# A stage border reordered: spikes counted by five comparisons, one fill moved to GpSimd, the first projections in two banks

## The chip, the cores and the metric

The kernel runs on one core of one Trainium2 chip. The metric is the device time of one launch in microseconds (us), as the median of several runs; lower is better. TensorE (PE) does the matrix products, VectorE (DVE), ScalarE (ACT) and GpSimd (POOL) work elementwise, and SyncE (SP) issues the transfers.

## What is computed

The input `x` has 8 sequences of 1024 tokens with 512 features. The cut reference:

```python
xn = layernorm(x)
# attention, 16 heads of 32, on xn
q, k, v = xn @ Wq.T, xn @ Wk.T, xn @ Wv.T
attn = softmax(q @ k.T * 512**-0.5) + rel_bias        # bias is added after the softmax
s = layernorm(attn @ v) * ln_gamma + ln_beta
# feed forward with spiking neurons, on xn
h = relu(xn @ W_fc.T) ** 2
y = h @ W_proj.T
mem = 0
for _ in range(5):
    mem = 0.9 * mem + y - (mem > 1)
    spikes += (mem > 1)
g = silu(spikes / 5)
out = x + s * g
```

## The kernel before, in words

The program has three stages, one after the other, each a block in which the five engines run their own queues in order; between blocks all engines meet.

**Weights** (`prepare_weights`). The weights are loaded, scaled and split in a high and a low half-precision part, so that three half-precision products (`TERMS`) stand for one of full precision.

**Feed forward** (`feed_forward`). The 8192 tokens go in 16 chunks (`NC`) of 512. In a chunk a loop over `f` (16 steps) runs a product with `w_fc` (L434, 12 matmuls of 512 columns), ScalarE's ReLU (L514), VectorE's square (L581), ScalarE's high part (L500), VectorE's low part (L586) and, two steps later, the product with `w_pr` into four banks (L447). ScalarE then copies `y` to memory (`copy_y`, L527). Beside that, the next chunk is loaded (`x_in`, L384), normalised, transposed and split into `xnT_part`, which SyncE stores to `xnT` in DRAM (L391), with a copy of the bias table (L399). The **recurrence** of a chunk takes 14 VectorE steps (`SpikingGate.recurrence`), each on all 2048 elements of a partition: L82, L84, L86, then L90, L92, L94 in turn, and last L98, the product of the spike count and the sigmoid. The sigmoid is three ScalarE instructions, `Exp`, `Ln`, `Exp` (L106, L110, L112). The recurrence of chunk c-1 runs in the steps `f` = 3 to 15 of chunk c; its sigmoid and its gate run in chunk c+1, and SyncE then stores the gate (L72). So at the end of the stage the sigmoid and gate of chunk 14 and the whole recurrence of chunk 15 are left over.

**Attention** (`attention`). The work goes in slots, one for each group of four heads of a sequence (32 slots, g = 0 to 31), each of 32 half steps `h`. A slot weighs the values of its own group (L978 scores transposed, L1042 ScalarE's exponential, L1294 GpSimd's bias, L993 product with the values) while the same slot prepares the next group: tiles of plain scores (L967), their row maximum on VectorE (`row_max`, L1101) and their exponential with row sums on ScalarE (`exp_sum`, L1048), 32 tiles a group. It also projects queries and keys two groups ahead (`project_qk`, L925, four units u = 0 to 3 of 12 matmuls of 512 columns) and values one group ahead (`project_v`, L908, two units of 48 matmuls of 128 columns). All projections go through one PSUM bank, `misc`: VectorE empties it (`take_qk`: L1135 writes the high part, L1137 the low one; `take_v`: L1107) before TensorE may start the next (`take_misc`, `last_use`). Once the four units of a group are read, SyncE spreads `nat` over `qst` and `kst` with 24 transfers (L853, six for each head), on which the score tiles wait (`stacked`).

Two slots in front, g = -2 and g = -1, fill this pipeline: slot -2 only projects queries and keys of group 0; slot -1 projects the values of group 0 and the queries and keys of group 1, and takes the first 26 tiles of group 0. What is left over of the spiking gate stands in them: ahead of the slots VectorE's four constants (`subT`, `before_key`, `identh`, and the ones in `kst`, L1255), the seven fills of `before_key` (L1258), for which TensorE waits before its first matmul (`CONSTS`), and the gate of chunk 14; in the slots the 13 steps of chunk 15 by the table

```python
RECURRENCES = {(-2, 17): (0, 1), (-2, 19): (2, 3), (-2, 23): (4, 5), (-2, 27): (6, 7), (-2, 31): (8,),
               (-1, 0): (9,), (-1, 2): (10,), (-1, 4): (11,), (-1, 5): (12,), (-1, 12): (13,)}
```

in which (g, h) says where a step stands in VectorE's queue. The order of every queue is the order of the code: each engine walks `slot` over its own steps. SyncE loads `xT` (L804), the normalised and transposed tokens of a whole sequence, at the start of the stage.

## Time and profile before

| | us |
|---|---|
| median of 3 runs (lowest to highest) | 3731.57 (3731.06 to 3733.22) |
| the profiled execution's own time | 3732.06 |
| its span | 3730.3 |
| PE busy | 3529.2 |
| DVE busy | 2738.0 |
| ACT busy | 2687.1 |
| POOL busy | 1577.9 |

The profile is one execution. Its span runs from the first to the last instruction; the execution's own time is 1.8 us longer. A busy TensorE is one with matmuls in flight, at whichever clock. Busy shares are averages over three stages, so they say little of any one of them; stretches of the span are read apart.

### The profile page before, as it was taken

What the parts mean: (1) busy time and instruction counts of PE and PEld (TensorE: products, weight loads), DVE (VectorE), ACT (ScalarE), POOL (GpSimd) and SP (SyncE); (2) the same over time, 40 slices, a digit from 0 to 9 for tenths busy, and PEclk for the clock granted to TensorE, in tenths of its full rate; (3) what the DMA queues carried; (4) which work ended last, traced back from release to release, by engine and by line L of the source; (5) the groups of instructions that cost most, each with busy time, mean ns of one, the idle gap of its engine ahead of it and who ended that gap; (6) DMA issues with size and microseconds to landing.
All of it is one profiled execution on the core that took longest, in us unless ns stands there. A gap on an engine that the chain in (4) does not pass through costs nothing.

```text
span 3730.3 us, 57349 instructions
## 1 busy us (share of the span) xinstructions
PE 3529.2 (95%) x20204; PEld 1498.2 (40%) x20204; DVE 2738.0 (73%) x4090; ACT 2687.1 (72%) x4941; POOL 1577.9 (42%) x898
## 2 busy tenths in 40 slices
PE   3999999999999996899999999999999999999985
PEld 1444444444444443343343343433433434334331
DVE  5376666666667667777877877778787787787776
ACT  4233333333433332999999999999999999999994
POOL 1000000000000000367677776776777767767766
PEclk6999999999999998999999999999999999999997
DMA  4011111111111102122232231232322322232221
GB/s 171 29 41 41 41 41 41 41 44 66 41 48 45 41 29 71 55 57 87 80 102 75 80 115 58 89 106 74 89 88 78 94 80 86 86 96 82 75 74 63
DMA packets 141421, 261.03 MB, mean 70 GB/s; under 512 B 19248, under 2 KB 52784, under 8 KB 140624
## 3 DMA queue, kind: packets, MB, share of 16 engines
q1 hardware_dynamic: 141136, 257.37, 21.9%
q8 instruction: 162, 2.65, 0.3%
q14 instruction: 123, 1.01, 0.1%
HBM read 155.77 MB, written 59.83 MB: 58 GB/s over the span
## 4 chain that ended last, share of the span: by engine, by line
ACT 38%; issue 18%; DVE 3%; PE 2%; ACTq 0%; POOL 0%; SPq 0%; DMA 0%; DVEq 0%
ACT recurrence_or_probs L1042 25%; ACT s_sb L1048 13%; PE st_ps L978 1%; PE acc L993 0%; DVE s_sb L1101 0%; ACTq L44 0%; PE s_ps L967 0%; DVE recurrence_or_probs L90 0%; PE misc L936 0%; PE misc L925 0%; DVE kst L1255 0%; DVE recurrence_or_probs L94 0%; DVE recurrence_or_probs L92 0%; DVE nat L1135 0%; DVE gate_or_tokens L1187 0%
## 5 line engine op out<-in xcount | busy, mean ns | idle before, releaser
L1101 DVE TENSOR_SCALAR_CACHE_REDUCE s_sb<-s_ps 128x1024 f32<-128x1024 f32 x1024 | 1244.6, 1222 | 424.0 <-PE s_ps L967 394.0
L1294 POOL TENSOR_TENSOR recurrence_or_probs<-recurrence_or_probs,toep 128x2048 f32<-128x2048 f32 (+3 forms) x384 | 1321.7, 3459 | 301.1 <-ACT recurrence_or_probs L1042 301.1
L1048 ACT ACTIVATE s_sb<-s_sb,nmax 128x1024 f32<-128x1024 f32 x1024 | 1270.1, 1240 | 7.2 <-DVE s_sb L1101 6.6
L1042 ACT ACTIVATE recurrence_or_probs<-st_ps 128x512 f32<-128x512 f32 x2048 | 1188.9, 678 | 16.3 <-PE st_ps L978 16.3
L978 PE MATMUL st_ps<-qst,kst 99*128 99x512 f16 x2048 | 677.7, 387 | 60.6 <-ACT recurrence_or_probs L1042 44.3
L434 PE MATMUL ps_fc<-xnT_part,w_fc 128*128 128x512 f16 x3072 | 706.1, 380 | 1.4 <-DVE xnT_part L573 1.4
L447 PE MATMUL ps_y<-w_pr,hid_part 128*128 128x512 f16 x3072 | 704.5, 379 | 0.0
L514 ACT ACTIVATE relu<-ps_fc 128x512 f32<-128x512 f32 x256 | 152.9, 597 | 733.1 <-PE ps_fc L434 733.1
L967 PE MATMUL s_ps<-kst,qst 96*128 96x512 f16 x2048 | 614.2, 381 | 8.9 <-DVE s_sb L1101 8.9
L1329 POOL MEMSET unit<- 128x16 f32 x1 | 0.1, 112 | 1408.3 <-POOLq L329 1408.3
L993 PE MATMUL acc<-recurrence_or_probs,val 128*32 128x512 f32 x4096 | 549.1, 609 | 4.6 <-POOL recurrence_or_probs L1294 4.6
L581 DVE TENSOR_TENSOR hid<-relu 128x512 f32<-128x512 f32 x256 | 177.1, 692 | 453.4 <-ACT relu L514 453.4
L978 PEld LDWEIGHTS st_ps<-qst,kst 99*128 99x128 f16 x2048 | 195.7, 98 | 707.7 <-ACT recurrence_or_probs L1042 598.9
L447 PEld LDWEIGHTS ps_y<-w_pr,hid_part 128*128 128x128 f16 x3072 | 300.6, 98 | 362.5
L434 PEld LDWEIGHTS ps_fc<-xnT_part,w_fc 128*128 128x128 f16 x3072 | 300.9, 98 | 351.8 <-issue 2.2
L1048 ACT ACTIVATION_READ_ACCUMULATOR s_sb<-s_sb,nmax 128x1 f32 x1024 | 298.4, 291 | 0.0
L500 ACT ACTIVATE hid_part<-hid 128x512 f16<-128x512 f32 x256 | 160.7, 628 | 160.8 <-DVE hid L581 160.8
L967 PEld LDWEIGHTS s_ps<-kst,qst 96*128 96x128 f16 x2048 | 199.8, 98 | 149.6 <-DVE s_sb L1101 11.2
L908 PE MATMUL misc<-w_v,xT 128*128 128x128 f16 x3072 | 194.8, 220 | 10.8 <-DVE val L1107 9.3
L925 PE MATMUL misc<-xT,w_q 128*128 128x512 f16 x768 | 190.1, 384 | 13.0 <-DVE before_key L1258 10.8
L908 PEld LDWEIGHTS misc<-w_v,xT 128*128 128x128 f16 x3072 | 184.2, 98 | 42.2 <-DVE val L1107 9.5
L925 PE MATMUL misc<-xT,w_k 128*128 128x512 f16 x768 | 188.2, 381 | 8.4 <-DVE nat L1137 6.6
(117 smaller groups left out, 2542.9 us busy)
## 6 DMA issues: line engine op xcount, KB each, us to landing
toep<-table_rows SPq DMA_DIRECT2D x32, 2048.0 KB, 8.1
qst<-nat SPq DMA_DIRECT2D x384, 64.0 KB, 2.0
kst<-nat SPq DMA_DIRECT2D x384, 64.0 KB, 2.0
x_in<-in_x SPq DMA_DIRECT2D x16, 1024.0 KB, 7.3
xnT<-xnT_part SPq DMA_DIRECT2D x32, 512.0 KB, 4.3
gate<-gate_or_tokens SPq DMA_DIRECT2D x16, 1024.0 KB, 4.3
xT<-xnT SPq DMA_DIRECT2D x32, 512.0 KB, 9.7
x_or_gate<-gate SPq DMA_DIRECT2D x64, 256.0 KB, 2.9
```

Of the source, the lines that this page charges most:

```text
L434: last = nc.tensor.matmul(ps_fc[:, f % 2, :], w["fc"][:, a, k, f * P:(f + 1) * P], xnT[:, par, b, k, :], start=(m == 0), stop=(m == 11))
L447: last = nc.tensor.matmul(ps_y[:, t, :], hid_part[:, f % 4, a, t * P:(t + 1) * P], w["pr"][:, b, f, :], start=(f == 0 and m == 0), stop=(f ...
L581: nc.vector.tensor_tensor(hid[:, f % 2, :], relu[:, f % 2, :], relu[:, f % 2, :], ALU.mult).then_inc(sq_done, 1)
L908: last = nc.tensor.matmul(misc[:, q * P:(q + 1) * P], xT[:, a, k, t * P:(t + 1) * P], w["v"][:, bb, k, s.next_hg * P:(s.next_hg + 1) * P], ...
L925: last = nc.tensor.matmul(misc[:], ww[:, a, k, s.ahead_hg * P:(s.ahead_hg + 1) * P], xT[:, bb, k, c * 512:(c + 1) * 512], start=(n == 0), ...
L967: last = nc.tensor.matmul(s_ps[:, i % 2, c * 512:(c + 1) * 512], qst[0:ROWS, par, j, st * P:(st + 1) * P], kst[0:ROWS, par, j, c * 512:(c ...
L978: nc.tensor.matmul(st_ps[:, j % 2, :], kst[:ROWS + SUBTRACTED, s.par, j, tb * P:(tb + 1) * P], qst[:ROWS + SUBTRACTED, s.par, j, half * 51 ...
L993: last = nc.tensor.matmul(acc[j * HD:(j + 1) * HD, :], val[:, par, tb, j * HD:(j + 1) * HD], prob[:, k % PROBS, j, :], start=(tb == 0), st ...
L1042: nc.scalar.activation(prob[:, k % PROBS, j, :], st_ps[:, j % 2, :], ACT.Exp).then_inc(p_done, 1)
L1048: nc.scalar.activation(s_sb[:, i % 4, :], s_sb[:, i % 4, :], ACT.Exp, bias=nmax[:, par, j, st:st + 1], scale=-1.0, accum_out=den[:, par, j ...
L1101: nc.vector.tensor_scalar(s_sb[:, i % 4, :], s_ps[:, i % 2, :], -1.0, None, ALU.mult, ALU.min, accum_out=nmax[:, par, j, st:st + 1]).then_ ...
L1294: nc.gpsimd.tensor_tensor(tile, tile, toep[:, par, :, at:at + width], ALU.add).then_inc(biased, 1)
```

## The change

- **Spikes by comparison.** The count of spikes of an element depends on `y` alone and grows with it. `spike_thresholds` finds, when the program is built, the five smallest `y` at which it reaches 1 to 5. `count_spikes` then takes five VectorE instructions on 2048 elements (one `tensor_scalar`, four `scalar_tensor_tensor`) in place of 13, and `gate_chunk` the last one.
- **Earlier in the feed forward.** The five stand in steps `f` = 3 to 7, the sigmoid in 8 to 10 and the gate in 13 of the same chunk; SyncE stores the gate of chunk c-1 in chunk c, not of chunk c-2. So only chunk 15 is left over, its five comparisons in slot -2 (`LAST_SPIKES`), its sigmoid at the end of slot -2, its gate in slot -1 (h = 15).
- **First x early.** `xT_first`, the tokens of the first sequence, is loaded in chunk 4 of the feed forward into a part of `gate_or_tokens` that is free then; the slots -2 and -1 project from it. `xT` is still loaded at the start of the stage, and slot 0 waits for it.
- **Two banks.** In slots -2 and -1 the projections alternate between `misc` and the bank `st_ps[:, 1]`, each with its own `last_use`. ScalarE (`prelude_takes`) writes the high part of `nat` and the values; VectorE keeps the low part.
- **Fill moved.** The ones in `kst` are written by GpSimd, behind `unit`; TensorE waits for them at slot 0 (`kst_ones`). One load of ScalarE's tables at the start of the stage goes.

The core of the diff (the declarations of tiles and semaphores are left out):

```diff
-    def recurrence(self, c, i):
+    def count_spikes(self, c, i):
         dve = self.nc.vector
-        base = c * self.STEPS
+        wait(dve, self.lif, c * self.STEPS + i)
         if i == 0:
             dve.wait_ge(self.y_ready, c * 4 + 4)
...
+            op = self.nc.vector.tensor_scalar(self.spikes, self.y, self.thresholds[0], None, ALU.is_ge)
         else:
...
+            op = self.nc.vector.scalar_tensor_tensor(self.spikes, self.y, self.thresholds[i], self.spikes, ALU.is_ge, ALU.add)
         op.then_inc(self.lif, 1)
+
+    def gate_chunk(self, c):
+        dve = self.nc.vector
+        dve.wait_ge(self.sig_done, c * 3 + 3)
+        wait(dve, self.gate_stored, c * 16)
+        self.nc.vector.scalar_tensor_tensor(self.gate, self.spikes, 1.0 / STEPS, self.sigmoids, ALU.mult, ALU.mult).then_inc(self.lif, 1)
...
@@ feed_forward, SyncE @@
-                if not (isinstance(c, int) and c < 2):
-                    spiking.store(sp, c - 2)
+                if c == 4:
+                    sp.wait_ge(xt_stored, 64)
+                    for half in range(2):
+                        for part in range(2):
+                            sp.dma_start(spiking.xT_first[:, part, :, half * 512:(half + 1) * 512],
+                                         d["xnT"].rearrange("c a (k p) s -> c a p k s", p=P)[half, part]).then_inc(first_loaded, 16)
+                if c >= 1:
+                    spiking.store(sp, c - 1)
@@ feed_forward, ScalarE @@
-                    if f < 3 and not (isinstance(c, int) and c < 2):
-                        spiking.sigmoid(c - 2, f)
+                    if 8 <= f < 11 and not first:
+                        spiking.sigmoid(c - 1, f - 8)
@@ feed_forward, VectorE @@
-                    if f == 3 and not (isinstance(c, int) and c < 2):
-                        spiking.recurrence(c - 2, 13)
-                    if f >= 3 and not first:
-                        spiking.recurrence(c - 1, f - 3)
+                    if 3 <= f < 3 + STEPS and not first:
+                        spiking.count_spikes(c - 1, f - 3)
+                    if f == 13 and not first:
+                        spiking.gate_chunk(c - 1)
@@ attention @@
+LAST_SPIKES = {(-2, 3): 0, (-2, 9): 1, (-2, 15): 2, (-2, 19): 3, (-2, 23): 4}
...
+        def prelude_bank(n):
+            return (st_ps[:, 1, :], 1, spiking.xT_first) if n % 2 else (misc, 0, spiking.xT_first)
@@ attention, TensorE @@
+                if s.g == 0:
+                    pe.wait_ge(kst_ones, 1)
+                    pe.wait_ge(qk_read, 8)
@@ attention, ScalarE @@
+            def prelude_takes(s, h):
+                if h in QUERY_KEYS and QUERY_KEYS[h][1]:
...
+                    act.wait_ge(qk_ps, n + 1)
+                    nc.scalar.activation(nat[:, which, 0, c * 512:(c + 1) * 512], prelude_bank(u)[0][:], ACT.Copy,
+                                         scale=SCALE if which == 0 else 1.0).then_inc(qk_hi, 1)
+                if h in VALUES and VALUES[h][1] and s.scores:
...
+                    act.wait_ge(v_ps, s.g * 2 + 2 + c + 1)
+                    nc.scalar.activation(val[:, 1 - s.par, c * 4:c * 4 + 4, :].rearrange("p a n -> p (a n)"), prelude_bank(c)[0][:],
+                                         ACT.Copy, scale=w["unscale"][:, 1:2]).then_inc(v_read, 1)
...
-                    if isinstance(s.g, int) and s.g == -1 and 3 <= k < 6:
-                        spiking.sigmoid(NC - 1, k - 3)
...
+                    if s.g < 0:
+                        prelude_takes(s, 2 * k)
+                    if s.g == -2 and k >= SLOT_STEPS - 3:
+                        spiking.sigmoid(NC - 1, k - SLOT_STEPS + 3)
...
-            load_exp_ln_tables(nc, act)
-            for i in range(3):
-                spiking.sigmoid(NC - 2, i)
@@ attention, VectorE @@
+                if g >= 0:
+                    dve.wait_ge(qk_ps, n + 1)
+                    nc.vector.tensor_scalar(hi, bank[:], factor, None, ALU.mult).then_inc(qk_hi, 1)
...
+                    if (s.g, h) in LAST_SPIKES:
+                        spiking.count_spikes(NC - 1, LAST_SPIKES[s.g, h])
+                    if (s.g, h) == (-1, 15):
+                        spiking.gate_chunk(NC - 1)
...
-            nc.vector.memset(kst[ROWS:ROWS + SUBTRACTED], 1.0).then_inc(consts, 1)
-            dve.wait_ge(consts, 4)
+            dve.wait_ge(consts, 3)
...
-            spiking.recurrence(NC - 2, 13)
@@ attention, GpSimd @@
             nc.gpsimd.memset(unit[:], 1.0).then_inc(unit_set, 1)
             pool.wait_ge(unit_set, 1)
+            nc.gpsimd.memset(kst[ROWS:ROWS + SUBTRACTED], 1.0).then_inc(kst_ones, 1)
+            pool.wait_ge(kst_ones, 1)
```

Three places of the queues, with the line numbers of either program.

VectorE, start of the attention stage, before (`nat` is the projected queries and keys, `recurrence_or_probs` the spiking gate's four buffers):

```order
L1254 CAST identh<-ident 128x128
L1255 MEMSET kst 3x8192
L1258 MEMSET before_key 128x7 [waits consts]
...
L98 SCALAR_TENSOR_TENSOR gate_or_tokens<-recurrence_or_probs 128x2048 [waits sig_done,lif,gate_stored,norm_loaded,const_loaded]
L1135 TENSOR_SCALAR nat<-misc 128x512 [waits qk_ps]
L1137 SCALAR_TENSOR_TENSOR nat<-misc,nat 128x512 [waits qk_hi]
L82 SCALAR_TENSOR_TENSOR recurrence_or_probs<-recurrence_or_probs 128x2048 [waits lif,y_ready]
L84 SCALAR_TENSOR_TENSOR recurrence_or_probs<-recurrence_or_probs 128x2048 [waits lif]
```

The same place in the changed program:

```order
L1308 CAST identh<-ident 128x128
L1311 MEMSET before_key 128x7 [waits consts]
...
L108 TENSOR_SCALAR recurrence_or_probs<-recurrence_or_probs 128x2048 [waits lif,y_ready,norm_loaded,const_loaded]
L110 SCALAR_TENSOR_TENSOR recurrence_or_probs<-recurrence_or_probs 128x2048 [waits lif]
L1190 SCALAR_TENSOR_TENSOR nat<-misc,nat 128x512 [waits qk_hi]
L110 SCALAR_TENSOR_TENSOR recurrence_or_probs<-recurrence_or_probs 128x2048 [waits lif]
L1190 SCALAR_TENSOR_TENSOR nat<-st_ps,nat 128x512 [waits qk_hi]
```

The fill of `kst`, the gate of chunk 14 and eight of the 13 steps are gone from between the constants and the first tile, as are the high parts.

TensorE, from its first projection to the first tile, before:

```order
L925 MATMUL misc<-xT,w_q 128x512 [waits xt_loaded0,consts]
L925 MATMUL misc<-xT,w_q 128x512 [waits xt_loaded1,qk_read]
L925 MATMUL misc<-xT,w_k 128x512 [waits qk_read]
L908 MATMUL misc<-w_v,xT 128x128 [waits qk_read]
L908 MATMUL misc<-w_v,xT 128x128 [waits v_read]
L967 MATMUL s_ps<-kst,qst 128x512 [waits stacked0]
```

and in the changed program (of each unit the first matmul; the others follow it without a wait, and the second unit has none at all):

```order
L958 MATMUL misc<-gate_or_tokens,w_q 128x512 [waits consts]
L958 MATMUL st_ps<-gate_or_tokens,w_q 128x512 x12
L958 MATMUL misc<-gate_or_tokens,w_k 128x512 [waits qk_read]
L958 MATMUL st_ps<-gate_or_tokens,w_k 128x512 [waits qk_read]
L940 MATMUL misc<-w_v,gate_or_tokens 128x128 [waits qk_read]
L940 MATMUL st_ps<-w_v,gate_or_tokens 128x128 [waits qk_read]
L1000 MATMUL s_ps<-kst,qst 128x512 [waits stacked0]
```

A unit now waits for the bank of the unit two before it, and no longer for a load.

ScalarE in the changed program, from the start of the stage to its first tiles (`s_sb`); all of it up to the values stood elsewhere or on VectorE before:

```order
L1106 ACTIVATE nat<-st_ps 128x512 [waits qk_ps]
L125 ACTIVATE recurrence_or_probs<-recurrence_or_probs 128x2048 [waits lif]
L129 ACTIVATE recurrence_or_probs<-recurrence_or_probs 128x2048 [waits sig_done]
L131 ACTIVATE recurrence_or_probs<-recurrence_or_probs 128x2048 [waits sig_done]
L1111 ACTIVATE val<-misc,unscale 128x512 [waits v_ps]
L1111 ACTIVATE val<-st_ps,unscale 128x512 [waits v_ps]
L1083 ACTIVATE s_sb,den<-s_sb,nmax 128x1024 [waits max_done] x8
L1106 ACTIVATE nat<-misc 128x512 [waits stacked3,stacked2,qk_ps,stacked1,stacked0]
```

The sigmoid now stands ahead of the first tiles' exponentials, and the high part of slot -1's first unit stands behind eight of them.

## Rows read from the trace of the kernel before

**Rows 1.** By stretch: us; PE, PEld, DVE, ACT, POOL busy; clock; DMA share; GB/s.
```profile
1200.00:1437.00 237.00, 236.11 (x1110) 109.01 (x1108) 158.22 (x165) 75.41 (x116) 0.00 (x0) 1.00 0.10 32
1437.00:1486.00 49.00, 21.66 (x140) 11.69 (x141) 43.95 (x34) 7.01 (x4) 0.11 (x1) 0.76 0.34 97
1486.00:1528.00 42.00, 28.84 (x114) 9.56 (x112) 38.91 (x64) 34.96 (x55) 1.49 (x6) 0.89 0.16 58
...
2000.00:2500.00 500.00, 488.02 (x3212) 199.56 (x3211) 397.67 (x676) 499.31 (x963) 362.21 (x208) 1.00 0.28 85
```

**Rows 2.** Timeline, start of the attention stage: start, us, engine, line, instruction, idle before.
```profile
1437.10 0.11 POOL L1329 MEMSET unit<- 128x16 f32 x1 [1408.26 <-POOLq L329]
1437.10 1.78 SPq L881 DMA_DIRECT2D far<-in_tableT  x4
...
1437.75 0.16 DVE L1254 CAST identh<-ident 128x128 f16<-128x128 f32 x1
1438.40 1.91 ACT L106 ACTIVATE recurrence_or_probs<-recurrence_or_probs 128x2048 f32<-128x2048 f32 x1
...
1439.68 6.88 DVE L1255 MEMSET kst<- 3x8192 f16 x1 [1.76 <-issue]
...
1446.90 4.63 PE L925 MATMUL misc<-xT,w_q 128*128 128x512 f16 x12 [10.79 <-DVE before_key L1258]
```

**Rows 3.** Timeline, the four query and key units of slot -2.
```profile
1452.29 0.69 DVE L1137 SCALAR_TENSOR_TENSOR nat<-misc,nat 128x512 f16<-128x512 f32 x1
...
1453.04 2.76 PE L925 MATMUL misc<-xT,w_q 128*128 128x512 f16 x12 [1.51 <-DVE nat L1137]
...
1458.75 1.22 DVE L86 TENSOR_SCALAR recurrence_or_probs<-recurrence_or_probs 128x2048 f32<-128x2048 f32 x1
...
1463.68 4.45 PE L925 MATMUL misc<-xT,w_k 128*128 128x512 f16 x12 [2.02 <-DVE nat L1137]
```

**Rows 4.** Timeline, from the last unit read to the first tiles.
```profile
1469.61 0.56 SPq L853 DMA_DIRECT2D qst<-nat  x1
...
1472.75 0.59 SPq L853 DMA_DIRECT2D kst<-nat  x1
...
1484.34 0.85 PE L967 MATMUL s_ps<-kst,qst 96*128 96x512 f16 x2
...
1486.19 1.22 DVE L1101 TENSOR_SCALAR_CACHE_REDUCE s_sb<-s_ps 128x1024 f32<-128x1024 f32 x1
```

**Rows 5.** Timeline, slot -1: the gate, and the row maxima of tiles 9 and 13.
```profile
1495.30 2.29 DVE L98 SCALAR_TENSOR_TENSOR gate_or_tokens<-recurrence_or_probs 128x2048 f32<-128x2048 f32 x1 [1.49 <-issue]
...
1503.72 1.21 DVE L1101 TENSOR_SCALAR_CACHE_REDUCE s_sb<-s_ps 128x1024 f32<-128x1024 f32 x1
...
1509.62 1.21 DVE L1101 TENSOR_SCALAR_CACHE_REDUCE s_sb<-s_ps 128x1024 f32<-128x1024 f32 x1
```

**Rows 6.** Timeline, a chunk border of the feed forward: x issued and first read.
```profile
1261.45 1.05 SPq L384 DMA_DIRECT2D x_in<-in_x  x1
...
1273.07 2.47 DVE L545 BATCH_NORM_STATS2 stats<-x_in 128x6 f32<-128x512 f32 x4
```

**Rows 7.** Groups by line: a ScalarE copy (min/median/max ns), a GpSimd fill; landing times.
```profile
L494 ACT ACTIVATE xnT_part<-ps_t x64: 591/591/597, 77.2 to 1335.6; 128x512 f16<-128x512 f32 x64
...
L182 POOL MEMSET ident<- 128x128 f32 x1 | 0.2, 205 | 0.3 <-POOLq L1380 0.3
...
qst<-nat SPq DMA_DIRECT2D x12, 64.0 KB, 2.0
...
x_in<-in_x SPq DMA_DIRECT2D x1, 1024.0 KB, 7.7
```

**Rows 8.** One VectorE tensor_scalar beside a GpSimd addition; its line: min/median/max ns.
```profile
1944.54 2.37 POOL L1294 TENSOR_TENSOR recurrence_or_probs<-recurrence_or_probs,toep 128x1024 f32<-128x1024 f32 x1 [2.61 <-ACT recurrence_or_probs L1042]
...
1946.05 0.88 DVE L1168 TENSOR_SCALAR frs<-fmv 128x4 f32<-128x4 f32 x1
...
L1168 DVE TENSOR_SCALAR frs<-fmv x16: 170/875/885, 1810.1 to 3714.7; 128x4 f32<-128x4 f32 x16
```

More of the change, by code:

```diff
@@ L11 @@
 from contextlib import ExitStack
+import numpy as np
 import concourse.bass as bass
@@ L32, with spike_thresholds, spikes @@
 TERMS = ((0, 0), (0, 1), (1, 0))
+def spike_thresholds():
+    f = np.float32
+    def spikes(y):
+        mem, count = f(0.0), 0
+        for _ in range(STEPS):
+            mem = f(f(f(f(BETA) * mem) + y) - f(1.0 if mem > f(1.0) else 0.0))
+            count += int(mem > f(1.0))
+        return count
+    found = []
+    for n in range(1, STEPS + 1):
+        low, high = f(0.0), f(2.0)
+        while np.nextafter(low, high) < high:
+            middle = f((low + high) / f(2.0))
+            low, high = (low, middle) if spikes(middle) >= n else (middle, high)
+        found.append(float(high))
+    return found
 def load_exp_ln_tables(nc, act):
@@ L522, in copy_y @@
             def copy_y(c):
-                wait(act, lif, (c - 1) * spiking.STEPS + 11)
+                wait(act, lif, (c - 1) * spiking.STEPS + STEPS)
                 for t in range(4):
@@ L690, in attention @@
         unit_set = sem("unit_set")
+        kst_ones = sem("kst_ones")
         const_loaded = sem("const_loaded")
@@ L859, in slot @@
                     load_xT(b + 1)
-                    spiking.store(sp, NC - 2)
                 elif s.scores:
@@ L907, in project_v @@
                     t = c * 4 + q
-                    last = nc.tensor.matmul(misc[:, q * P:(q + 1) * P], xT[:, a, k, t * P:(t + 1) * P],
+                    last = nc.tensor.matmul(bank[:, q * P:(q + 1) * P], x[:, a, k, t * P:(t + 1) * P],
                                             w["v"][:, bb, k, s.next_hg * P:(s.next_hg + 1) * P],
```

82 lines of the change are left out of this document (36 added, 46 removed).

## The prediction

> **What bounds the kernel now.** I read the stretches first [rows 1]. In the feed forward TensorE is busy 236 of 237 us at its full clock, while VectorE and ScalarE have room. In the slots ScalarE is busy 499.3 of 500 us. Between the two lie some 90 us (1437 to 1528) in which neither is full: TensorE is busy 21.7 of the first 49 us, ScalarE 7.0, VectorE 44.0. So at the border VectorE is the bound, and from about 1528 ScalarE works through a fixed list of exponentials. Whatever starts that list earlier shortens the program by as much; nothing else in this change can.
>
> Then I read the timeline of those 90 us for the chain that ends last. TensorE's first matmul stands still for 10.8 us until VectorE's constants are written, of which the ones in `kst` take 6.88 us, behind a gap of 1.76 us in which VectorE waits for nothing that the profile shows [rows 2]. Then each projection of slot -2 waits until VectorE has emptied the one bank, and VectorE meets that between steps of the recurrence of 2.3 us [rows 3]. The last unit is read at about 1469.6, when SyncE issues the first spread transfer [rows 4]. The first tile could start when the sixth of these has landed: issued at 1472.75 [rows 4] with 2.0 us to landing [rows 7], so at 1474.8. It starts at 1484.34, because the second value unit, in front of it on TensorE, waits for VectorE's `take_v` behind five more recurrence steps. Its row maximum starts at 1486.19 [rows 4]. In slot -1 the gate (1495.30, 2.29 us) holds the row maxima up, and the maximum of tile 9 starts at 1503.72, that of tile 13 at 1509.62 [rows 5]: from there 5.90 us for four tiles and one unit.
>
> **The feed forward: nothing.** VectorE loses nine instructions of a chunk; TensorE is the bound, so this is worth 0. The sigmoid moves from steps 0 to 2 to steps 8 to 10, where each instruction of 1.91 us [rows 2] stands beside three passes over 512 elements of about 0.6 us, as the copy's [rows 7]: 3.7 us of a step of 5.2 (24 matmuls, two units of the 2.76 us of [rows 3] that overlap a little). The gate's store now stands in SyncE's queue in front of the next chunk's transfers and waits for step 13; these wait for step 14 anyway. It would bite through x: x is issued at 1261.45, lands 7.7 us later [rows 7], and is read at 1273.07 [rows 6], a slack of 3.9 us; a gate that is issued a step earlier has mostly landed by then. The four loads of `xT_first` stand behind x and the table in chunk 4 and nobody waits for them before the border. All of it is hidden by TensorE's matmuls; if not, it costs at most a few us for each of 15 chunks.
>
> **The new start.** The fill of `kst` goes to GpSimd. No row shows this fill there. Its two fills of other sizes are 0.11 us for 16 elements [rows 2] and 0.205 us for 128 [rows 7], thus 0.83 ns an element and 6.9 us for 8192, what VectorE took. The lower end is the row nearest in size, 0.2 us; the upper end is 7 ns an element as in the small fill, 57 us. I take 6.9 us, since the slope of two rows leaves the fixed part out. It starts behind `unit` at about 1437.4 and ends at 1444.3. TensorE waits for it only at slot 0, near 1505.
>
> It is not free, though. In this trace a `tensor_scalar` on four elements, which takes 0.17 us at its shortest, took 0.88 us when it came at 1946.05, inside a GpSimd addition that began at 1944.54 and took 2.37 us: both ended at 1946.9. The median of that line is 0.875 us [rows 8]. So VectorE can be held until a GpSimd instruction ends. Whether a fill, which reads nothing, holds it too, and which VectorE instructions, no row shows. The ends are no hold and a hold to 1444.3, and I take the hold: the cast of `identh`, at 1437.75 in this trace [rows 2], comes 0.3 us after the fill starts and so would stand until 1444.3. Then come the fills of `before_key` and at 1444.8 the first matmul, not at 1446.9: the fill is off VectorE's queue but VectorE still waits for it. The Trainium skill (SBUF — State Buffer, section "Who interferes with whom") says that casts, copies and `tensor_scalar` in the modes that use two ports shut GpSimd out or are shut out by it, whichever comes first, for the whole instruction. By that rule the sum is the one I take; without it the rival below.
>
> **Slot -2 from there.** Lengths: a unit 4.63 us at the low clock [rows 2], 2.76 at the high one [rows 3]; high part on ScalarE 0.59 [rows 7]; low part 0.69, the first comparison 1.22 [rows 3], the others 2.29 as the gate's form [rows 5]; VectorE's instructions follow each other some 0.08 us closer. Unit 0 ends at 1449.4, its high part at 1450.1, its low part at 1450.8 (the first two comparisons fit ahead of it). From here VectorE alternates comparison and low part: 1453.0, 1453.6, 1455.9, 1456.5, 1458.8, 1459.4. TensorE is ahead of it, unit 1 ending at 1452.2, unit 2 at 1455.0, unit 3 at 1457.8. So the last unit is read at 1459.4, in place of 1469.6: 10.2 us.
>
> **To the first maximum.** The sixth transfer lands 3.15 + 2.0 us later; the first tile takes 0.85 [rows 4], with semaphores 6.3 us to the maximum, at 1465.7. Neither value unit waits for VectorE now, since the second has its own bank. Before it was at 1486.2: 20.5 us. The sigmoid (three of 1.91 us from 1458.8, to 1464.6) and the values come ahead of the first exponential on ScalarE, which begins at about 1467.7, 0.8 us behind its maximum, and then keeps pace at the 1.15 us of a maximum.
>
> **Slot -1.** From the first maximum to that of tile 9: second tile behind half a value unit 1.85 us, seven more at 1.15, the last maximum 1.15, high part 0.75, low part 0.65, gate 2.25: 14.7 us, and about 0.5 for TensorE at its low clock; 15.2 in place of 17.5, which gives 2.3. From there on the high part sits behind exponentials on ScalarE, and the low part waits for it: four maxima 4.57, high part 0.75 after the last exponential, low part 0.65 make 6.0 in place of 5.90, for four groups a loss of 0.4. Rows, table and keys of slot 0 keep their distance, as they hang on the same steps.
>
> **Sum:** 10.2 + 10.3 + 2.3 - 0.4 = 22.4 us, all on the path. The profiled execution took 3732.06 us; less 22.4 it is 3709.7. It lies 0.5 us above the median of the runs, so the forecast is 3709 us.
>
> **The rivals.**
> *No hold, or a late one (27 in 100).* If the cast passes, VectorE's next tie is the load of `far`: four issues in 1.78 us from 1437.10 [rows 2] and, taken like the spread transfers, 2.0 us to land [rows 7], 1440.9. Then VectorE alone sets the rest, 13.2 us of comparisons and low parts to 1454.1 or so, 27.5 us gained: 3704. If only the first comparison is held, to 1444.4, the last read comes at 1457.2: 3707. For it: nothing in the trace shows a fill that holds VectorE. Against: rows 8.
> *TensorE becomes the bound (17 in 100).* Unit 3 took 4.45 us after a pause of 2.0 us [rows 3], and the mean clock is 0.76 from 1437 to 1486 [rows 1]. If all four units run at the low clock, 5.1 us each, with a high and a low part behind the last, the last read is near 1466.5, 7 us later: 3716. Against: without pauses between units, unlike before, the clock should rise after the first.
> *The feed forward pays (7 in 100).* If the gate's store delays x beyond its 3.9 us of slack and VectorE's two steps of lead, 1 us in each of 15 chunks gives 3724.
> *GpSimd's fill is long (4 in 100), the slower end.* Place: VectorE's cast at 1437.75 and all behind it. Each us above 6.9 costs one. At 29 us the gain is gone; at 57 us, the upper end, the time is 3759, slower than before. Without the hold it decides from slot 0 only, at 67 us. Against: the 128-element fill, eight times the elements for 0.09 us more.
> *The change does nothing:* only if the exponentials were not the bound from 1528; 499.3 of 500 us [rows 1] speak against it. I leave it 2 in 100, which stands with "same".
>
> **The numbers.** The forecast itself has 43 in 100, the likeliest: 3709. The range of 8 in 10 takes in the case without hold (3704, and an error of 1.5 us) and TensorE at the low clock (3716 and 1.5): 3702 to 3718. What a measurement can tell from no change is 0.2%, 7.5 us. Faster by more than that are the forecast, the first two rivals and part of the third: 0.93. Within it 0.04, slower 0.03.
>
> **What the profile would show.** The attention stage still starts near 1437. GpSimd's fill of 3x8192 reads about 6.9 us, and VectorE's cast reads about 6.5 us, or stands beside it at 0.16 (then no hold). TensorE's first projection starts near 1444.8 (no hold: near 1440); the first spread transfer is issued near 1459.4, the first maximum starts near 1465.7, that of tile 9 near 1481, and the first exponential of slot 0 comes near 1505.5, before at 1528.0. In the feed forward the steps stay at 5.2 us. Wrong would be: a first exponential of slot 0 that comes much earlier without the time following, a wait for `kst_ones` in slot 0, or a stage that starts later than 1438.

## The result, and the profile after

| | before | after |
|---|---|---|
| median, us (lowest to highest) | 3731.86 (3731.06 to 3733.22) | 3709.88 (3709.67 to 3713.54) |
| the profiled execution: own time, span | 3732.06, 3730.3 | 3713.54, 3711.8 |

Each median is of four runs. The ratio is 0.9943, with a 95% interval of 0.993 to 0.9955: 22.0 us less, where 22.4 were forecast. The profiled execution is the slowest of four, 3.7 us above their median, and its span is 18.5 us shorter than before's. So I compare stages by their distance from the attention stage's first instruction, and come back to the 3.7 us at the end.

The stretches after, in the columns of [rows 1]:

```profile
1200.00:1437.00 237.00, 237.00 (x1115) 109.51 (x1113) 106.64 (x141) 79.68 (x119) 0.00 (x0) 1.00 0.09 32
1437.00:1486.00 49.00, 31.36 (x189) 15.38 (x189) 35.95 (x44) 22.83 (x33) 7.03 (x2) 0.86 0.41 119
1486.00:1528.00 42.00, 35.20 (x218) 17.09 (x217) 32.21 (x55) 37.60 (x70) 11.56 (x16) 0.88 0.30 84
2000.00:2500.00 500.00, 487.60 (x3143) 195.95 (x3136) 397.38 (x674) 499.34 (x965) 367.32 (x208) 1.00 0.29 88
```

VectorE lost a third of its work in the feed forward (158.2 to 106.6 of 237 us) and the stage is no shorter, since TensorE fills all of it, as before. In the long middle ScalarE is at 499.3 of 500 us in both. All of the gain lies in the 90 us between.

The timeline at the start of the stage, after (start, us, engine, line, instruction, idle before). It answers to [rows 2, 3]:

```profile
1438.35 6.92 POOL L1383 MEMSET kst<- 3x8192 f16 x1
1438.36 0.48 DVE L1306 MEMSET subT<- 128x512 uint32 x1 [6.19 <-PEq L348]
...
1438.84 6.52 DVE L1308 CAST identh<-ident 128x128 f16<-128x128 f32 x1
1445.42 0.13 DVE L1311 MEMSET before_key<- 128x7 f32 x7
1445.58 1.23 DVE L108 TENSOR_SCALAR recurrence_or_probs<-recurrence_or_probs 128x2048 f32<-128x2048 f32 x1
1445.69 4.49 PE L958 MATMUL misc<-gate_or_tokens,w_q 128*128 128x512 f16 x12 [8.50 <-DVE before_key L1311]
...
1450.01 2.75 PE L958 MATMUL st_ps<-gate_or_tokens,w_q 128*128 128x512 f16 x12
1450.21 0.60 ACT L1106 ACTIVATE nat<-misc 128x512 f16<-128x512 f32 x1 [12.29 <-PE misc L958]
1450.84 0.69 DVE L1190 SCALAR_TENSOR_TENSOR nat<-misc,nat 128x512 f16<-128x512 f32 x1 [1.71 <-ACT nat L1106]
1451.45 2.28 DVE L110 SCALAR_TENSOR_TENSOR recurrence_or_probs<-recurrence_or_probs 128x2048 f32<-128x2048 f32 x1
...
1459.25 0.68 DVE L1190 SCALAR_TENSOR_TENSOR nat<-st_ps,nat 128x512 f16<-128x512 f32 x1
...
1459.96 0.56 SPq L884 DMA_DIRECT2D qst<-nat  x1
```

The cast that took 0.16 us now reads 6.52: it begins 0.5 us after GpSimd's fill and ends with it, at 1445.36 against 1445.27. VectorE's own fill of `subT`, which begins with GpSimd's, reads 0.48 us, as in before. Of the low parts (L1190) only the first waits, 1.71 us for ScalarE's copy behind the first unit; from 1450.8 VectorE goes without a pause from comparison to low part.

The row maxima of slot -1 (L1152) after, and what stands between them (answers to [rows 4, 5]):

```profile
1465.18 0.60 PE L1000 MATMUL s_ps<-kst,qst 96*128 96x512 f16 x2 [3.22 <-DMA kst<-nat]
...
1465.83 1.23 DVE L1152 TENSOR_SCALAR_CACHE_REDUCE s_sb<-s_ps 128x1024 f32<-128x1024 f32 x1 [5.90 <-PE s_ps L1000]
...
1468.68 1.22 DVE L1152 TENSOR_SCALAR_CACHE_REDUCE s_sb<-s_ps 128x1024 f32<-128x1024 f32 x1 [1.62 <-PE s_ps L1000]
...
1474.23 2.59 PE L958 MATMUL misc<-gate_or_tokens,w_q 128*128 128x512 f16 x6
...
1477.29 1.22 DVE L1152 TENSOR_SCALAR_CACHE_REDUCE s_sb<-s_ps 128x1024 f32<-128x1024 f32 x1 [1.59 <-PE s_ps L1000]
...
1478.44 1.22 DVE L1152 TENSOR_SCALAR_CACHE_REDUCE s_sb<-s_ps 128x1024 f32<-128x1024 f32 x1
...
1480.42 0.69 DVE L1190 SCALAR_TENSOR_TENSOR nat<-misc,nat 128x512 f16<-128x512 f32 x1 [0.74 <-ACT nat L1106]
1481.02 2.28 DVE L118 SCALAR_TENSOR_TENSOR gate_or_tokens<-recurrence_or_probs 128x2048 f32<-128x2048 f32 x1
...
1483.22 1.22 DVE L1152 TENSOR_SCALAR_CACHE_REDUCE s_sb<-s_ps 128x1024 f32<-128x1024 f32 x1
```

The first tile now waits for the transfer and no longer for a value unit in front of it. But VectorE waits 1.62 and 1.59 us for TensorE in this stretch.

The milestones, as distances in us from the stage's first instruction (worked out from the timelines; "rest" runs from the first exponential of slot 0, L1077 on `st_ps`, to the end of the span). The experiments' rows belong to the next section:

| kernel | first projection | first spread transfer | first row maximum | maximum of tile 9 | first exponential of slot 0 | rest |
|---|---|---|---|---|---|---|
| before | 9.80 | 32.51 | 49.09 | 66.62 | 90.86 | 2202.34 |
| after | 7.50 | 21.77 | 27.64 | 45.03 | 69.91 | 2203.70 |
| fill_late | 1.15 | 17.46 | 23.34 | 40.82 | 65.16 | 2204.44 |
| fill_after_cast | 1.15 | 21.20 | 27.06 | 45.61 | 71.79 | 2203.83 |
| fill_vector | 9.89 | 24.18 | 30.05 | 47.45 | 72.32 | 2203.63 |
| fill_pieces | 1.53 | 18.18 | 24.04 | 41.44 | 66.31 | 2200.57 |
| one_bank | 7.51 | 25.51 | 34.49 | 50.93 | 75.26 | 2199.76 |
| vector_takes | 7.50 | 23.66 | 29.96 | 47.69 | 72.62 | 2200.93 |
| compare_alone | 9.79 | 28.87 | 37.50 | 52.93 | 77.18 | 2202.00 |
| late_no_far | 1.15 | 13.70 | 19.99 | 38.22 | 62.56 | 2199.96 |
| x_late | 8.21 | 23.35 | 29.64 | 47.84 | 72.71 | 2202.82 |
| late_x_late | 8.22 | 22.20 | 28.06 | 46.55 | 72.17 | 2200.29 |

### The profile page after: what moved, and what is told of

The parts are those of the page before. It is cut to its first block, busy times and chain, and to the rows that moved or that the text cites. A ratio compares the mean times of both kernels' runs of the same rounds, so it can differ in the third digit from the quotient of the medians.

```text
span 3711.8 us, 57226 instructions
## 1 busy us (share of the span) xinstructions
PE 3524.2 (95%) x20204; PEld 1495.8 (40%) x20204; DVE 2447.3 (66%) x3951; ACT 2691.8 (73%) x4950; POOL 1584.3 (43%) x899
## 4 chain that ended last, share of the span: by engine, by line
ACT 38%; issue 19%; DVE 2%; PE 1%; POOL 1%; ACTq 0%; SPq 0%; DMA 0%; DVEq 0%; POOLq 0%
ACT recurrence_or_probs L1077 25%; ACT s_sb L1083 13%; POOL recurrence_or_probs L1346 1%; ACTq L69 0%; PE st_ps L1011 0%; PE s_ps L1000 0%; DVE s_sb L1152 0%; PE misc L958 0%; PE acc L1026 0%; DVE recurrence_or_probs L110 0%; DVE identh L1308 0%; DVE gate_or_tokens L1240 0%; DVE frs L1228 0%; DVE frs L1226 0%; DVE gate_or_tokens L1243 0%
## 5 line engine op out<-in xcount | busy, mean ns | idle before, releaser
L1152 DVE TENSOR_SCALAR_CACHE_REDUCE s_sb<-s_ps 128x1024 f32<-128x1024 f32 x1024 | 1244.5, 1221 | 431.2 <-PE s_ps L1000 401.4
L1077 ACT ACTIVATE recurrence_or_probs<-st_ps 128x512 f32<-128x512 f32 x2048 | 1189.5, 679 | 17.8 <-PE st_ps L1011 17.8
L1000 PE MATMUL s_ps<-kst,qst 96*128 96x512 f16 x2048 | 614.3, 381 | 13.4 <-DVE s_sb L1152 9.9
L1026 PE MATMUL acc<-recurrence_or_probs,val 128*32 128x512 f32 x4096 | 547.4, 607 | 7.8 <-POOL recurrence_or_probs L1346 7.8
L940 PE MATMUL misc<-w_v,xT 128*128 128x128 f16 x2976 | 187.2, 219 | 0.0
L958 PE MATMUL misc<-xT,w_k 128*128 128x512 f16 x720 | 175.1, 379 | 1.8 <-DVE nat L1190 0.2
L613 DVE TENSOR_TENSOR hid_part<-hid,hid_part 128x512 f16<-128x512 f32 x256 | 175.1, 684 | 0.1
```

The source lines that it names most:

```text
L613: nc.vector.tensor_tensor(hid_part[:, f % 4, 1, :], hid[:, f % 2, :], hid_part[:, f % 4, 0, :], ALU.subtract).then_inc(lo_done, 1)
L940: last = nc.tensor.matmul(bank[:, q * P:(q + 1) * P], x[:, a, k, t * P:(t + 1) * P], w["v"][:, bb, k, s.next_hg * P:(s.next_hg + 1) * P], ...
L1000: last = nc.tensor.matmul(s_ps[:, i % 2, c * 512:(c + 1) * 512], qst[0:ROWS, par, j, st * P:(st + 1) * P], kst[0:ROWS, par, j, c * 512:(c ...
L1026: last = nc.tensor.matmul(acc[j * HD:(j + 1) * HD, :], val[:, par, tb, j * HD:(j + 1) * HD], prob[:, k % PROBS, j, :], start=(tb == 0), st ...
L1077: nc.scalar.activation(prob[:, k % PROBS, j, :], st_ps[:, j % 2, :], ACT.Exp).then_inc(p_done, 1)
L1152: nc.vector.tensor_scalar(s_sb[:, i % 4, :], s_ps[:, i % 2, :], -1.0, None, ALU.mult, ALU.min, accum_out=nmax[:, par, j, st:st + 1]).then_ ...
```

## The experiments

Each is an edit of the changed kernel, except compare_alone. Each time is a median of five runs; the kernel before, run beside them, gave 3731.27 (with the four that move or cut the fill), 3731.38 (with one_bank, vector_takes, compare_alone and late_no_far) and 3732.51 (with x_late and late_x_late). The theory in all of them is the prediction's: GpSimd's fill holds VectorE, and the gain is made of the parts that the prediction sums. A median and the distance to the first exponential do not move by the same amount: against after (compare_alone against before) they differ by 2 us or less in eight of the ten, by 2.3 in x_late and by 3.2 in fill_late. So both are given where they disagree.

### Does the fill hold VectorE? The fill behind the first comparison

```diff
+            pool.wait_ge(spiking.lif, (NC - 1) * spiking.STEPS + 1)
             nc.gpsimd.memset(kst[ROWS:ROWS + SUBTRACTED], 1.0).then_inc(kst_ones, 1)
```

> GpSimd's fill of kst waits until VectorE's first comparison of the last chunk is done; nothing else differs from the change. Theory (the fill holds VectorE's cast, since it holds instructions of the kind of casts and tensor_scalars, and the held cast delays TensorE's first matmul): the cast reads 0.16 us, TensorE's first projection starts 2 to 3 us after the stage's first instruction (7.5 us in the change), the four-operand comparisons beside the fill read 2.29 us as ever, the last unit is read 4 to 5 us earlier, and the kernel takes 3705 us. Rival 1 (a GpSimd fill holds every VectorE instruction): a comparison beside the fill reads up to 9 us and the time is 3709 or more. Rival 2 (TensorE or the load of far binds next): the cast is free but less than 2 us come of it, 3708.

Measured: 3708.37 us (3704.04 to 3710.97), ratio 0.9937 (0.9924 to 0.9949). Its timeline:

```profile
1437.55 0.16 DVE L1308 CAST identh<-ident 128x128 f16<-128x128 f32 x1
1437.78 0.13 DVE L1311 MEMSET before_key<- 128x7 f32 x7
...
1438.05 2.76 PE L958 MATMUL misc<-gate_or_tokens,w_q 128*128 128x512 f16 x12 [2.14 <-DVE before_key L1311]
...
1441.72 1.23 DVE L108 TENSOR_SCALAR recurrence_or_probs<-recurrence_or_probs 128x2048 f32<-128x2048 f32 x1 [3.81 <-DMA far<-in_tableT]
1442.98 2.29 DVE L110 SCALAR_TENSOR_TENSOR recurrence_or_probs<-recurrence_or_probs 128x2048 f32<-128x2048 f32 x1
1443.07 6.92 POOL L1384 MEMSET kst<- 3x8192 f16 x1 [6.06 <-DVE recurrence_or_probs L108]
...
1445.93 4.02 PE L958 MATMUL misc<-gate_or_tokens,w_k 128*128 128x512 f16 x12 [2.53 <-DVE nat L1190]
```

With no fill beside it the cast is back at 0.16 us. TensorE starts 6.4 us earlier, and its first unit, after a pause of 2.1 us in place of 8.5, takes 2.76 us in place of 4.49. The comparisons (L110) beside the fill read 2.29, as without it. The next wait is the one the prediction named: the load of `far`, 3.81 us. The first exponential comes 4.75 us earlier than after, near the 5 of the theory, and the profiled executions differ by 5.3 us in span. The medians differ by 1.5 us only: 3708.4, where the theory said 3705 and the second rival (another wait takes its place) 3708. The distances at the border speak for the theory and the time for that rival's price. fill_late's five runs spread over 7 us and after's four over 4, so how much of the 5 us reaches the end these runs leave uncertain; the fill in pieces, below, comes to 3705.6.

### The fill behind the constants

```diff
+            pool.wait_ge(consts, 3)
             nc.gpsimd.memset(kst[ROWS:ROWS + SUBTRACTED], 1.0).then_inc(kst_ones, 1)
```

> GpSimd's fill waits until the cast is done, so it starts about 1 us into the stage. Theory (cast and tensor_scalar are both held): the cast reads 0.16 us and TensorE starts some 3 us into the stage, but the first comparison, a tensor_scalar, is held until the fill ends, some 8 us into the stage; last unit read about 1 us earlier than in the change, 3709. Rival (only the cast is held, a comparison is not): the first comparison reads 1.22 us beside the fill, and the time is that of the late fill, 3705.

Measured: 3709.91 us (3708.38 to 3714.06), ratio 0.9944 (0.9931 to 0.9956).

```profile
1437.33 0.16 DVE L1308 CAST identh<-ident 128x128 f16<-128x128 f32 x1
...
1437.62 6.92 POOL L1384 MEMSET kst<- 3x8192 f16 x1 [0.83 <-DVE before_key L1311]
...
1441.51 4.11 DVE L108 TENSOR_SCALAR recurrence_or_probs<-recurrence_or_probs 128x2048 f32<-128x2048 f32 x1 [3.82 <-DMA far<-in_tableT]
1445.65 2.29 DVE L110 SCALAR_TENSOR_TENSOR recurrence_or_probs<-recurrence_or_probs 128x2048 f32<-128x2048 f32 x1
...
1448.60 5.09 PE L958 MATMUL misc<-gate_or_tokens,w_k 128*128 128x512 f16 x12 [5.42 <-DVE nat L1190]
```

Now the cast is free and the first comparison is held: 4.11 us in place of 1.23, 2.9 more; it starts when the fill, which ends at 1444.54, has 3.0 us to go. The fills of `before_key` (0.13 us) reach into GpSimd's fill and are not held. So the hold falls on the cast or on the `tensor_scalar`, whichever meets the fill, and neither on fills nor on a `scalar_tensor_tensor` with two operands in the buffer. That is what the Trainium skill (SBUF — State Buffer, section "Who interferes with whom") says of these kinds: cast and `tensor_scalar` can take the port pair that GpSimd uses, and a VectorE instruction with two inputs meets only a GpSimd instruction that reads. The rows here agree. What the early start won on TensorE is then lost: it stands still for 5.42 us behind VectorE, and its third unit takes 5.09 us. The first spread transfer comes 0.6 us earlier than after and the first exponential 1.9 later; the time is the same.

### The fill back on VectorE

```diff
+            nc.vector.memset(kst[ROWS:ROWS + SUBTRACTED], 1.0).then_inc(kst_ones, 1)
             dve.wait_ge(consts, 3)
+            dve.wait_ge(kst_ones, 1)
...
-            nc.gpsimd.memset(kst[ROWS:ROWS + SUBTRACTED], 1.0).then_inc(kst_ones, 1)
-            pool.wait_ge(kst_ones, 1)
```

> The fill goes back to VectorE ahead of the fills of before_key, as in the kernel before; all other parts of the change stay. Theory (moving the fill was worth only what VectorE's own fill ends later than the held cast, since VectorE waits for it either way): the first projection starts 9.8 us into the stage in place of 7.5, and the kernel takes 2 us more than the change, 3712. Rival (the fill's move is a main part of the gain): 6.9 us more, 3717.

Measured: 3713.31 us (3712.87 to 3714.91), ratio 0.9952 (0.9939 to 0.9964).

```profile
1439.73 6.88 DVE L1309 MEMSET kst<- 3x8192 f16 x1 [1.76 <-issue]
1446.75 0.23 DVE L1313 MEMSET before_key<- 128x7 f32 x7
```

The gap of 1.76 us is back with the instruction, so it is part of its price on VectorE: 8.6 us. Moving the fill was worth 3.4 us (3713.3 less 3709.9), or 2.4 by the distances of the spread transfer and the first exponential, and not the 8.6, since the cast waits for it on the other engine.

### The fill in eight pieces

```diff
-            nc.gpsimd.memset(kst[ROWS:ROWS + SUBTRACTED], 1.0).then_inc(kst_ones, 1)
-            pool.wait_ge(kst_ones, 1)
+            for par in range(2):
+                for j in range(HG):
+                    nc.gpsimd.memset(kst[ROWS:ROWS + SUBTRACTED, par, j], 1.0).then_inc(kst_ones, 1)
+            pool.wait_ge(kst_ones, 8)
```

(TensorE waits for 8 as well.)

> GpSimd's fill in eight pieces of 1024 elements, started as in the change. Theory (a VectorE instruction is held until the GpSimd instruction that was there first ends, and then gets in): cast and first comparison are held for at most one piece each, 0.9 us; about 3705. Rival (GpSimd's next piece gets in ahead of the held VectorE instruction): the cast reads some 7 us as in the change and the time is 3710.

Measured: 3705.59 us (3704.54 to 3707.94), ratio 0.993 (0.9917 to 0.9944).

```profile
1437.69 8.36 POOL L1385 MEMSET kst<- 3x1024 f16 x8
...
1438.17 0.55 DVE L1308 CAST identh<-ident 128x128 f16<-128x128 f32 x1
...
1442.76 1.51 DVE L108 TENSOR_SCALAR recurrence_or_probs<-recurrence_or_probs 128x2048 f32<-128x2048 f32 x1 [3.84 <-DMA far<-in_tableT]
```

The same elements are written from the same moment on, in 8.36 us in place of 6.92, and the hold is 0.39 us on the cast and 0.28 on the comparison: VectorE is held by one instruction of GpSimd, and gets in between two. With the first experiment this settles the hold: it is the length of the single fill that costs, not its bytes.

### One bank again

```diff
-            return (st_ps[:, 1, :], 1, spiking.xT_first) if n % 2 else (misc, 0, spiking.xT_first)
+            return misc, 0, spiking.xT_first
```

> The change, but all projections of the slots -2 and -1 in misc; ScalarE still makes the high parts. Theory (each unit then waits for its predecessor's high and low part, and the second value unit for ScalarE's copy behind the sigmoid): the first spread transfer is issued some 26 us into the stage in place of 21.8, the first row maximum starts some 5.5 us later, and the kernel takes 3715 us. Rival (VectorE is the bound of slot -2 in any case, so the second bank is worth nothing): 3710.

Measured: 3713.94 us (3713.52 to 3715.65), ratio 0.9954 (0.994 to 0.9967). The first spread transfer comes at +25.51, 3.7 us later than after, and the first row maximum 6.85 later, because the second value unit is in front of the first tile again. At the first exponential 5.35 us are left and in the time 4.1. In this trace TensorE does not stand still in front of the first tile; the third line is the second row maximum:

```profile
1468.15 2.74 PE L940 MATMUL misc<-w_v,gate_or_tokens 128*128 128x128 f16 x24 [2.68 <-ACT val L1111]
...
1471.37 1.50 PE L940 MATMUL misc<-w_v,gate_or_tokens 128*128 128x128 f16 x24
...
1473.35 1.22 DVE L1152 TENSOR_SCALAR_CACHE_REDUCE s_sb<-s_ps 128x1024 f32<-128x1024 f32 x1 [0.54 <-PE s_ps L1000]
```

The half value unit between the first two tiles takes 1.50 us here, at a granted clock of 1.00, and the second maximum comes 1.78 us behind the first. That is used below.

### High parts and values on VectorE

```diff
-                    if s.g < 0:
-                        prelude_takes(s, 2 * k)
...
-                if g >= 0:
-                    dve.wait_ge(qk_ps, n + 1)
-                    nc.vector.tensor_scalar(hi, bank[:], factor, None, ALU.mult).then_inc(qk_hi, 1)
+                dve.wait_ge(qk_ps, n + 1)
+                nc.vector.tensor_scalar(hi, bank[:], factor, None, ALU.mult).then_inc(qk_hi, 1)
```

(and `take_v` in slot -1 likewise.)

> The change, but VectorE makes the high parts and the values of the slots -2 and -1 itself, from the two banks. Theory (VectorE is the bound of slot -2 and gets four passes of 0.7 us more there, partly in its idle time, and one before the second maximum): first spread transfer 2 to 2.5 us later, time 3713. Rival (the copies through ScalarE cost in slot -1 what they save in slot -2): 3710 or less.

Measured: 3712.47 us (3711.95 to 3717.47), ratio 0.9951 (0.9938 to 0.9963). Four `tensor_scalar` of 0.69 us stand in VectorE's row again; the milestones move by 1.9 (spread), 2.3 (first maximum) and 2.7 us (first exponential), the time by 2.6.

### The comparisons alone, in the kernel before

```diff
-RECURRENCES = {(-2, 17): (0, 1), (-2, 19): (2, 3), (-2, 23): (4, 5), (-2, 27): (6, 7), (-2, 31): (8,),
-               (-1, 0): (9,), (-1, 2): (10,), (-1, 4): (11,), (-1, 5): (12,), (-1, 12): (13,)}
+RECURRENCES = {(-2, 17): (0,), (-2, 19): (1,), (-2, 23): (2,), (-2, 27): (3,), (-2, 31): (4,), (-1, 12): (5,)}
```

(with `count_spikes` for the 13 steps; fill, bank, x, and the order of gate and sigmoid as before.)

> The kernel before with the five comparisons in place of the 13 steps and nothing else: the same places in the queues, one bank, VectorE's fill, late x; the gate of chunk 14 and its sigmoid still in the attention stage. Theory (VectorE's recurrence is the longest part of the border): first spread transfer 28 to 29 us into the stage in place of 32.5, first row maximum at 36.5 in place of 49.1, 3718 us, thus more than half of the whole gain. Rival (waits of the one bank and the fill take its place): gain under 6 us, 3726.

Measured: 3718.15 us (3715.61 to 3718.83), ratio 0.9962 (0.9949 to 0.9974). This one part brings 13.2 us (3731.38 less 3718.15), where the whole change brings 22.0. Each projection still waits for VectorE:

```profile
1457.47 2.76 PE L940 MATMUL misc<-xT,w_k 128*128 128x512 f16 x12 [1.51 <-DVE nat L1152]
```

### x late

`xT_first` is left out of the feed forward, and the slots -2 and -1 project from `xT`:

```diff
-            return (st_ps[:, 1, :], 1, spiking.xT_first) if n % 2 else (misc, 0, spiking.xT_first)
+            return (st_ps[:, 1, :], 1, xT) if n % 2 else (misc, 0, xT)
```

> The change without the early load of the first x: the slots -2 and -1 project from xT, which is loaded at the start of the stage, and TensorE waits for its halves; the fill still holds the cast. Theory (the load lands about when the held cast lets TensorE start, so the early load is worth almost nothing in the change): first projection 0 to 1.5 us later than 7.5 us into the stage, time 3710 to 3711. Rival (the early load is a main part of the gain): 3714 or more.

Measured: 3710.35 us (3709.38 to 3714.64), ratio 0.9943 (0.9931 to 0.9956).

```profile
1445.48 5.28 PE L951 MATMUL misc<-xT,w_q 128*128 128x512 f16 x12 [9.21 <-DMA xT<-xnT]
```

TensorE starts at +8.21 in place of +7.50, and is released by the load, no longer by the held cast; its first unit takes 5.28 us in place of 4.49. The first spread transfer comes 1.6 us later than after and the first exponential 2.8, but the medians differ by 0.5 us only. So beside the hold the early x is worth between nothing and some 3 us, and these runs can't say which.

### Both waits away: the fill late, and the wait for far late

VectorE waits for `far`, `gamma` and `beta` ahead of its first comparison only because they are loaded in that stage. Nothing in slots -2 and -1 reads them, so the wait moves to slot 0:

```diff
                 if h == SUM_VALUES and s.main:
+                    if s.g == 0:
+                        dve.wait_ge(const_loaded, 64)
+                        dve.wait_ge(spiking.norm_loaded, 32)
                     take_values(s)
...
-            dve.wait_ge(const_loaded, 64)
-            dve.wait_ge(spiking.norm_loaded, 32)
...
+            pool.wait_ge(spiking.lif, (NC - 1) * spiking.STEPS + 1)
             nc.gpsimd.memset(kst[ROWS:ROWS + SUBTRACTED], 1.0).then_inc(kst_ones, 1)
```

> The late fill, and VectorE's wait for the loads of far, gamma and beta moved from the head of the stage to the first use of far in slot 0. Theory (with the hold gone, the wait for far is VectorE's next tie, 3.8 us): first comparison starts 1 us into the stage, first spread transfer near 14.5 us in place of 17.5, and some 3 us less than the late fill: 3703 to 3705. Rival (TensorE's low clock gives it back): under 1 us less.

Measured: 3701.88 us (3701.24 to 3706.17), ratio 0.9923 (0.9911 to 0.9936). **This version beats both kernels**, the changed one by 8.0 us. Against fill_late it is 6.5 us, where 3 were expected; at the first exponential it is 2.6. fill_late is the one whose median stands highest above its distances, so the 2.6 may be the better measure of the wait for `far`.

```profile
1438.52 1.23 DVE L108 TENSOR_SCALAR recurrence_or_probs<-recurrence_or_probs 128x2048 f32<-128x2048 f32 x1
...
1438.73 2.76 PE L958 MATMUL misc<-gate_or_tokens,w_q 128*128 128x512 f16 x12 [2.14 <-DVE before_key L1314]
...
1439.88 6.92 POOL L1385 MEMSET kst<- 3x8192 f16 x1 [2.18 <-DVE recurrence_or_probs L108]
1441.33 2.75 PE L958 MATMUL st_ps<-gate_or_tokens,w_q 128*128 128x512 f16 x12
```

VectorE and TensorE both run almost without a pause from 1438.5; the first spread transfer goes out at +13.70, 8.1 us ahead of after's.

### The same with x late

The edit of x_late in this version:

> As late_no_far (late fill, late wait for far), but with xT loaded at the start of the stage in place of the early x. Theory (without the hold the load is TensorE's tie): the first projection starts near 8 us into the stage in place of 1.2, the kernel takes 3710 us, 8 more than with the early x. Rival (VectorE's comparisons bound slot -2 whatever TensorE does): 3704 or less.

Measured: 3710.31 us (3709.54 to 3713.64), ratio 0.9942 (0.9929 to 0.9956).

```profile
1446.16 4.20 PE L951 MATMUL misc<-xT,w_q 128*128 128x512 f16 x12 [9.21 <-DMA xT<-xnT]
```

The whole gain of the last version is gone again, 8.4 us, and 9.6 at the first exponential. So undoing the early x costs 0.5 us of time (2.8 at the first exponential) with the hold in place and 8.4 (9.6) with both of VectorE's waits away. The held cast and the load of x release TensorE within 0.7 us of each other, so that with the one in place the other hardly shows. The early x with the hold away but the wait for `far` in place was not tried.

## Why the prediction was right

By its own steps, before to after, each as a difference of the distances in the table:

| step | forecast | measured |
|---|---|---|
| feed forward | 0 | 0: TensorE 237.0 of 237 us |
| last unit read (first spread transfer) | 10.2 | 10.7 |
| from there to the first maximum | 10.3 | 10.7 |
| first maximum to tile 9's | 2.3 | 0.1 |
| tile 9's to the first exponential of slot 0 | -0.4 | -0.6 |
| sum | 22.4 | 20.9 |

The feed forward came as said. The working has VectorE lose nine instructions of a chunk; it is eight (14 before, five comparisons and the gate after), which changes nothing, as TensorE is the bound there.

**The hold.** It was taken from one row of another pair of instructions [rows 8] and carried 5 us of the forecast. Four runs bear it out: 6.4 us on the cast (6.52 for 0.16), 2.9 on the comparison, 0.4 and 0.3 by pieces, none with the fill later. The fill's length, 6.92 us, is the 6.9 that two smaller fills gave [rows 2, 7]; the bounds of 0.2 and 57 us were much too wide, but named by their rows.

**Slot -2.** TensorE's start at +7.5 (forecast 7.7), the first unit 4.49, and VectorE's alternation of comparison and low part came as written, 2.8 us a pair. TensorE ran the later units at 2.75 us, at a granted clock of 1.00 from 1450 to 1457.7, so the rival that TensorE becomes the bound did not come.

**The step that failed** is "Slot -1": 15.2 us from the first maximum to tile 9's, measured 17.39. Its pieces show where. The second tile came 2.85 us behind the first, forecast 1.85. The next seven maxima took 9.76 us, forecast 8.05 (seven by 1.15): one of them waited 1.59 us for TensorE, which was taking 2.59 us over half a projection. The rest, 4.78 us of last maximum, high part, low part and gate, was forecast at 4.80. So 2.7 us went where I had allowed 0.5 for TensorE at its low clock:

```profile
1465.83:1468.68 2.85, 2.85 (x27) 2.21 (x25) 1.23 (x2) 0.85 (x2) 0.00 (x0) 0.58 0.33 78
...
1474.00:1477.00 3.00, 3.00 (x10) 1.10 (x8) 1.71 (x4) 2.98 (x6) 0.00 (x0) 0.58 0.44 102
```

These are two short stretches of after, in the columns of [rows 1]: TensorE is busy all of both, at a granted clock of 0.58, thus mostly at 1.2 GHz. It had stood still for 3.22 us in front of the first tile, waiting for the transfer. For the distance of the first two maxima the experiments settle the cause, as the same half value unit stands between them: 1.78 us at a clock of 1.00 (one_bank, with no pause in front of the first tile), 2.85 at 0.58 (after), 3.41 at 0.50 (late_no_far). The forecast's 1.85 is the value at the full clock. For the 1.71 us in the next seven maxima it is in part argued: the half projection took 2.59 us, and the next one, at 1477.53, 1.46; the difference of 1.1 us is most of the wait of 1.59. But no run shows these seven at the full clock throughout; they took 9.65 to 10.36 us in after and the nine experiments with its feed forward. From the first maximum to tile 9's TensorE was busy 11.3 of 17.5 us before and 13.4 of 17.4 after, at a clock of 0.80 in both. A bound that moves from VectorE to TensorE has to be priced at the clock at which TensorE will find itself, and I priced it mostly at the other.

**What made up for it.** The sum at the first exponential is 1.5 us short. Of that 0.7 comes back at once: the second pair of slot 0's exponentials follows the first by 3.49 us, before by 4.21, which I had not looked at. Nothing more came back in the profiled execution: its "rest" is 1.4 us longer than before's and its attention stage begins 1.1 us later, so that it took 3713.5 us, where the working gives 3709.7 for a profiled execution. That the median lies 0.9 us from the forecast is therefore partly luck: what made up for the short sum in the other executions no profile shows.

**A sign of being wrong.** The prediction named a stage that starts later than 1438, and after's starts at 1438.19. In the nine experiments with the same feed forward it starts between 1436.68 and 1437.94, so the rows do not lay this on the reordered feed forward; why this execution is late is open.

**The rivals.** "No hold" was priced at 3704, and fill_late is that case: its first exponential came 4.75 us ahead of after's (5 forecast), its time was 3708.4, from 3704.0 to 3711.0. The price of the mechanism was right at the border; the median shows only a part of it, and 3708.4 is not the 3704 of the rival. "GpSimd's fill is long" (6.92 us) and "the feed forward pays" (TensorE 237.0 of 237 us) are out. Beyond the rivals, what bounds the border is the pair of waits that late_no_far takes away; the prediction saw the one for `far` and put it only under the case without a hold.

**What stays open.** The "rest" from slot 0's first exponential to the end varies from 2199.8 to 2204.4 us over the twelve profiled executions, in no order that fits an edit. After's profiled execution has one of the longer ones, and its attention stage starts 1.1 us later than before's; both may be part of the 3.7 us by which it lies above the median. Near the end, after has a group of eight matmuls (L1026) that take 1.94 us where most others take 1.06 or 1.07:

```profile
3661.15 1.94 PE L1026 MATMUL acc<-recurrence_or_probs,val 128*32 128x512 f32 x8
```

fill_late has two such groups, fill_pieces none in that stretch, and before has one too. Whether TensorE's clock in the last slot makes the difference was not tried, so this is not more than a place to look. For the same reason a difference of one to three us between two medians is not read here by itself.

## What to carry to other kernels

- An instruction moved to GpSimd is off VectorE's queue but not out of its way: the cast and the `tensor_scalar` here waited until its end, though it only writes. Put such a fill where VectorE runs fills or instructions with two inputs, or cut it in pieces of about a microsecond, as fill_pieces does.
- At a stage border, list the waits that end at nearly the same time. Here the load of `far`, the held cast and the load of x ended 4.8, 7.2 and 8.2 us into the stage: undoing the early x cost 0.5 us (2.8 at the first exponential) with the others in place and 8.4 (9.6) without them.
- When an engine stops being the bound, price the next one at the clock it will have there: the distance of the first two row maxima was 1.78 us at a granted clock of 1.00, 2.85 at 0.58 and 3.41 at 0.50.
